# Eight chained sublayers on one core: the norm of a sublayer's first step moved into the sublayer ahead

## The reference

```python
x = x + jnp.tanh(g_xattn[0]) * _L0_xattn_ref(_layernorm(x), ctx_2048, ...)   # A: 32 heads of 8, q and k normed
x = x + jnp.tanh(g_ffn[0])   * _L0_ffn_ref(_layernorm(x), ...)               # B: Hadamard, 8-bit inputs, ternary weights
x = x + jnp.tanh(g_xattn[1]) * _L1_xattn_ref(_layernorm(x), ctx_2048, ...)   # C: norms again, inputs rounded to fp8, two attentions
x = x + jnp.tanh(g_ffn[1])   * _L1_ffn_ref(_layernorm(x), ...)               # D: attention whose tanh(attn @ Wo.T @ A) scales a low-rank gate
x = x + jnp.tanh(g_xattn[2]) * _L2_xattn_ref(_layernorm(x), ctx_2048, ...)   # E: quantised attention over all 1024 keys
x = x + jnp.tanh(g_ffn[2])   * _L2_ffn_ref(_layernorm(x), ...)               # F: 8 experts, 2 chosen, and a shared one
x = x + jnp.tanh(g_xattn[3]) * _L3_xattn_ref(_layernorm(x), ctx_2048, mask)  # G: attention without projections
x = x + jnp.tanh(g_ffn[3])   * _L3_ffn_ref(_layernorm(x), ...)               # H: Hadamard, SiLU gate, Hadamard
```

## Time and profile before

| what | value |
|---|---|
| median of three runs | 1738.55 us (1736.21 to 1738.9) |
| the profiled execution | 1734.91 us, of which the span of the core is 1733.1 us |
| mean granted TensorE clock | 0.823 of full speed |
| TensorE matmul busy | 1374.4 us, 79% of the span |
| VectorE busy | 1217.3 us, 70% |
| ScalarE busy | 958.6 us, 55% |
| GpSimd busy | 277.4 us, 16% |
| DMA | 38.09 MB, mean 22 GB/s |

### The profile page before, as it was taken

The page is one execution under the profiler, slowest core; times in us unless marked ns, Lnnn a source line. Parts: engine busy times, 40 slices in busy tenths (PEclk is TensorE's granted clock), DMA queues, the critical chain, the costliest instruction groups (busy, mean ns, idle before and its releaser), DMA issues.

```text
span 1733.1 us, 26920 instructions
## 1 busy us (share of the span) xinstructions
PE 1374.4 (79%) x9109; PEld 962.1 (56%) x9122; DVE 1217.3 (70%) x2705; ACT 958.6 (55%) x2865; POOL 277.4 (16%) x347
## 2 busy tenths in 40 slices
PE   4775665388898897996799995788888899977886
PEld 3653444156675665675567762444444457765664
DVE  4786887679889999874454418888888885644432
ACT  2552677387687786881456513667766772323121
POOL 0000322143353443442000000000000000000000
PEclk8995787699899999997999998556555558978888
DMA  5302000100000000004200000000000001000000
GB/s 196 144 4 97 1 0 1 52 1 7 1 1 6 1 3 3 1 1 159 98 1 1 1 1 19 1 2 1 0 0 0 1 1 49 0 1 0 1 0 24
DMA packets 13581, 38.09 MB, mean 22 GB/s; under 512 B 2201, under 2 KB 8866, under 8 KB 10802
## 3 DMA queue, kind: packets, MB, share of 16 engines
q1 hardware_dynamic: 13490, 36.99, 5.7%
HBM read 35.94 MB, written 1.05 MB: 21 GB/s over the span
## 4 chain that ended last, share of the span: by engine, by line
PE 47%; DVE 35%; ACT 8%; issue 7%; POOL 2%; DVEq 0%; DMA 0%; ACTq 0%; POOLq 0%; another core or an unknown queue 0%
PE PS L2287 4%; PE PS L2267 4%; PE PS L2899 4%; DVE small L2407 3%; DVE work L1134 2%; DVE work L2417 2%; PE PS L1874 2%; PE PS L1803 2%; PE PS L690 2%; PE PS L1367 2%; PE PS L1905 2%; DVE work L1161 2%; PE PS L2934 2%; PE PS L1375 2%; DVE small L1183 1%
## 5 line engine op out<-in xcount | busy, mean ns | idle before, releaser
L2407 DVE TENSOR_REDUCE small<-PS 128x1 f32<-128x1024 f32 x128 | 156.3, 1221 | 18.1 <-PE PS L2267 12.9
L2352 ACT ACTIVATE work<-PS,small 128x1024 f32<-128x1024 f32 x128 | 154.8, 1209 | 23.9 <-DVE small L2409 23.0
L212 POOL TENSOR_TENSOR rstd<-moments,eps 128x1 f32<-128x1 f32 x56 | 13.5, 240 | 923.2 <-DVE moments L192 923.2
L2287 PE MATMUL PS<-ident_b,work 128*128 128x128 bf16 x1024 | 122.6, 295 | 41.9 <-DVE work L2417 35.5
L1250 POOL TENSOR_TENSOR small<-small,minus_half 128x4 f32<-128x4 f32 x96 | 108.9, 1135 | 263.1 <-ACT small L1290 262.8
L1375 PE MATMUL PS<-late 128*128 128x512 f16 x384 | 103.6, 402 | 58.5 <-DVE work L1177 34.7
L2267 PE MATMUL PS<-early,work 64*128 64x512 bf16 x256 | 121.9, 575 | 4.6 <-ACT work L2352 2.8
L2287 PEld LDWEIGHTS PS<-ident_b,work 128*128 128x128 bf16 x1024 | 92.3, 133 | 47.2 <-DVE work L2417 36.9
L1340 ACT ACTIVATE work<-PS,small 128x128 f32<-128x128 f32 x256 | 90.3, 364 | 48.0 <-DVE small L1184 48.0
L2345 ACT COPY work<-PS 128x512 f32<-128x512 f32 x128 | 75.0, 586 | 68.6 <-PE PS L2287 68.6
L1375 PEld LDWEIGHTS PS<-late 128*128 128x128 f16 x384 | 36.1, 101 | 112.0 <-DVE work L1177 46.7
(11 more groups left out here) (407 smaller groups left out, 3436.4 us busy)
## 6 DMA issues: line engine op xcount, KB each, us to landing
late<-in_C_proj SPq DMA_DIRECT2D x1, 4096.0 KB, 12.4
ctxT<-in_ctxT SPq DMA_DIRECT2D x24, 128.0 KB, 2.6
late<-in_C_q SPq DMA_DIRECT2D x1, 2048.0 KB, 9.1
late<-in_C_qx SPq DMA_DIRECT2D x1, 2048.0 KB, 12.6
late<-in_F_w SPq DMA_DIRECT2D x2, 1024.0 KB
...
```

The costliest lines, as they stand in the source:

```text
L2287: last = nc.tensor.transpose(bank(g, 1).bitcast(BF16)[:, b * P:(b + 1) * P], E_[g]["pb"][:, b * P:(b + 1) * P], ident_b[:])
L2352: nc.scalar.activation(E_[g]["e"], banks(g, 2), ACT.Exp, scale=small[:, g, h:h + 1], bias=small[:, g, 48 + h:49 + h], accum_out=small[:, g ...
L2407: ch.link(nc.vector.tensor_reduce(small[:, g, 80:81], banks(g, 2), AX.X, ALU.max))
```

## The change

The norm of the first step is moved from the beginning of B, C, D, F, G and H into the last step of the sublayer ahead. There it is called with `STEPS` in place of the step, which stands for batches 0 and 1 of X and for the flags of the next sublayer. E's norm stays where it is. In detail:

- A: the buffers are cleared before x is waited for, and TensorE projects the context before it transposes x. In A's last slot the order is now `out_T` of the first half, statistics, `out_T` of the second half, xn, and then the rounding of B's weights.
- B: `C_prepare` goes into slot 5, the statistics of C's first norm into slot 6, the first pass and the second norm into slot 7; `C_proj_low` of parts 14 and 15 goes ahead of the last add. GpSimd's powers go with them. TensorE transposes C's x before it waits for the parts of C's weights.
- C: ahead of the loops only the three roundings of batch 0 are done (k, q, v); those of batch 1 are in slot 0 between `normed_k` and `normed_q`. TensorE waits for each input by itself. In the later steps the roundings go batch by batch too, k, q, v.
- D: the first norm is in slots 6 to 8 of C's last step. The transposes of the fold come before the transposes of x, its copy behind the copies of xT, and its products behind `project_qk`. The waits for the cleared buffers (`prepared`) move to where they are used. `D_xb` lies elsewhere.
- F: its first norm is in slots 8 and 10 of E's last step. G: the statistics of batches 0 to 5 are taken at the head of F's last body, those of 6 and 7 between xn 1 and xn 2. H: its norm is between G's adds.

```diff
-        BEFORE[0, 4] = A_prepare
+        BEFORE[0, 4] = lambda dve, ch: (A_prepare(dve, ch), dve.wait_ge(x_in, 16))
...
             def first(ch):
+                project_kv(0, 0)
                 turn_x(0, 0)
-                projections(0, 0)
+                project_q(0, 0)
                 turn(0, 0, 0)
...
                 if ahead:
                     normed(ch, i, u + 1)
-                elif layers > 1:
-                    B_quantise_weights(dve, ch, PS[:, PREP[0], 0:3])
                 out_T(i, u, 0)
...
+                if not ahead and layers > 1:
+                    norm_stats(ch, STEPS)
                 out_T(i, u, 1)
+                if not ahead and layers > 1:
+                    for b in range(G):
+                        normed_batch(dve, STEPS, b)
+                    B_quantise_weights(dve, ch, PS[:, PREP[0], 0:3])
...
             def first(ch):
-                norm_stats(ch, 0)
-                for u in range(G):
-                    normed_batch(dve, 0, u)
                 norm_stats(ch, 0, [G])
...
+                    if n == 5:
+                        C_prepare(ch)
+                    if n == 6:
+                        norm_stats(ch, STEPS)
+                    if n == 7:
+                        C_again(dve, ch, STEPS)
                 if ahead:
                     quantise_x(ch, i, u + 1)
...
                     if n == 3:
                         C_proj_scale(dve, ch)
+                    if n == NB - 1:
+                        C_twice_normed(dve, STEPS, 0)
                     if n >= 4:
                         for m in (0, 1):
                             C_proj_low(dve, 4 * (n - 4) + m)
+                    if n == NB - 1:
+                        for m in (14, 15):
+                            C_proj_low(dve, m)
                 dve.wait_ge(B_down.sem, B_down.nth(i, u))
                 add_to_x(dve, ch, i * G + u, PS[:, B_DOWN, 0:D], small[:, g, 11:12])
-                if not ahead and layers > 2:
-                    for m in (14, 15):
-                        C_proj_low(dve, m)
...
+                    if n == NB - 2:
+                        norm_gpsimd(pool, ch, STEPS)
+                    if n == NB - 1:
+                        C_again_power(pool, ch, 0)
                     for m in range(3):
                         C_low(pool, 3 * n + m)
...
-        BEFORE[2, 4] = lambda dve, ch: C_prepare(ch)
-        BEFORE[2, 1] = lambda pe, ch: (pe.wait_ge(C_low_done.sem, C_low_done.nth(0, GROUPS - 1)),
+        BEFORE[2, 1] = lambda pe, ch: (C_turn_x(pe, 0), pe.wait_ge(C_low_done.sem, C_low_done.nth(0, GROUPS - 1)),
                                        pe.wait_ge(C_proj_low_done.sem, C_proj_low_done.nth(0, PAIRS - 1)))
...
                 if last_step(i):
+                    if layers > 3:
+                        if n == DEPTH:
+                            norm_stats(ch, STEPS)
+                        if n == DEPTH + 1:
+                            D_normed(dve, ch, STEPS)
+                        if n == DEPTH + 2:
+                            D_normed_again(dve, STEPS, 0)
                     return
...
+                if n == 0:
+                    for k, m in enumerate((2, 0, 3)):
+                        activations(ch, 1, m)
+                        dve.wait_ge(C_xs.sem, C_xs.nth(0, 3 + k))
                 if 1 <= n % UNITS <= G:
                     activations(ch, n % UNITS - 1, 1)
                 if 11 <= n < 17:
-                    m, g = divmod(n - 11, G)
+                    g, m = divmod(n - 11, 3)
                     if m == 0:
                         dve.wait_ge(xT_ready.sem, xT_ready.at(i + 1, g))
-                    activations(ch, g, (2, 3, 0)[m])
+                    activations(ch, g, (2, 0, 3)[m])

             def first(ch):
-                norm_stats(ch, 0)
-                again(ch, 0)
-                twice_normed(ch, 0)
-                for n in (2, 3, 0):
-                    for g in range(G):
-                        dve.wait_ge(xT_ready.sem, xT_ready.at(0, g))
-                        activations(ch, g, n)
+                dve.wait_ge(C_low_done.sem, C_low_done.nth(0, GROUPS - 1))
+                dve.wait_ge(xT_ready.sem, xT_ready.at(0, G - 1))
+                for n, m in enumerate((2, 0, 3)):
+                    activations(ch, 0, m)
+                    dve.wait_ge(C_xs.sem, C_xs.nth(0, n))
...
                 if r == 0:
-                    pe.wait_ge(C_xs.sem, C_xs.nth(i, 8 * (u // UNITS) + 4 + g))
+                    pe.wait_ge(C_xs.sem, C_xs.nth(i, 8 * (u // UNITS) + 3 * g))
...
+                if s == 0:
+                    act.wait_ge(D_folded, 1)
+                    nc.scalar.copy(D_turned_o.rearrange("p a b -> p (a b)"), PS[:, GATE:GATE + 2, :].rearrange("p a b -> p (a b)")).then_inc(D_folded, 1)
...
+                if s == 0:
+                    act.wait_ge(D_folded, 3)
+                    nc.scalar.copy(D_oa.rearrange("p a b -> p (a b)"), PS[:, TBANK_D, 0:64]).then_inc(D_folded, 1)
...
             def turn_x(s):
-                if s >= 2:
-                    pe.wait_ge(x_done.sem, x_done.nth(s - 1, -1))
+                if s != 1:
+                    pe.wait_ge(x_done.sem, x_done.nth(max(s - 1, 0), -1))
...
+            def turn_fold():
+                for k in range(KC):
+                    for tt in range(4):
+                        last = nc.tensor.transpose(PS[:, GATE + k, tt * P:(tt + 1) * P], wD["o"][:, tt, k * P:(k + 1) * P], ident[:])
+                last.then_inc(D_folded, 1)
...
                 if s is not None:
                     project_qk(s)
+                if s == 0:
+                    fold()
...
-            pe.wait_ge(D_folded, 4)
+            turn_fold()
             D_slots(None, slot)
...
                 if last_step(i):
+                    if n == E_DEPTH and layers > 5:
+                        norm_stats(ch, STEPS)
+                    if n == E_DEPTH + 2 and layers > 5:
+                        for b in range(G):
+                            normed_batch(dve, STEPS, b)
                     return
...
             def body(ch, i, s):
-                if s is not None:
+                if i is not None and s is not None:
                     norm_vector(dve, ch, s)
+                if s is None and layers > 6:
+                    G_stats_of(ch, range(6))
...
         def G_vector(dve, ch):
             for h in range(2):
                 dve.wait_ge(rstd_ready.sem, rstd_ready.nth(0, HALF * h + HALF - 1))
                 for b in range(HALF * h, HALF * h + HALF):
+                    if b == 2:
+                        dve.wait_ge(x_done.sem, x_done.nth(0, -1))
+                        G_stats_of(ch, range(6, NB))
...
                     add_to_x(dve, ch, b, PS[:, b, 0:D], G_sum[:, b:b + 1])
+                    if b == G - 1 and layers > 7:
+                        dve.wait_ge(x_done.sem, x_done.nth(0, b))
+                        norm_stats(ch, STEPS)
+                    if b == HALF and layers > 7:
+                        for u in range(G):
+                            normed_batch(dve, STEPS, u)
```

195 lines of the change are left out of this document (107 added, 88 removed).

## The result

The changed kernel took 1692.74 us in the median of four runs (1688.6 to 1700.96), the kernel before 1737.38 in four (1734.19 to 1738.9); the ratio is 0.9752, with an interval of 0.9726 to 0.9777. So 44 us are gone, where 26 were forecast, and the time lies 8 us under the low end of the range, 1701. The profiled execution took 1691.2 us.

A forecast was written before the change was run, and what follows sets the result against it. It took a chain through all engines (47% TensorE, 35% VectorE) to bound the kernel, with waits where sublayers begin. Ten terms summed to -26.2 us, giving 1712 us; own range 1705 to 1719, stretched for rivals to 1701 to 1725.

The forecast's parts named there:

- C's order in the later steps: Middle of C: instructions called the same apart from the order of rounding, with no term for it in the sum.
- A's start: Start of A: buffers cleared before x lands, A_kv's landing late next; -2.9 us.
- A to B: Border of A and B: out_T waits for TensorE and B's weight rounding waits behind it; +0.8 us, bounds -1 to +3.
- B's slots: B's slots 5 to 7: moved constants and norms mostly covered by VectorE's idle time; +1.0 us, bounds 0 to +5.9.
- rival 1: Steps taking in moved work: covers fail, the work costs its length; +12 to +13 us, 1725 us; chance 0.10.
- B to C: Border of B and C: norm done before, three roundings ahead of C's first q; -11.2 us, bounds -8 to -12.5.
- C to D: Border of C and D: q and k projection starts earlier, fold's products ahead of the scores; -7.4 us.
- E's last step: E's last step: VectorE sets the pace, so the added norm is hardly covered; +1.6 us, bounds +0.7 to +2.5.
- E to F: Border of E and F: TensorE's idle time ahead of its first transpose goes; -2.9 us, bounds -3.3 to -2.
- F to G: Border of F and G: statistics of six batches go ahead, first transpose at 1540.6; -4.2 us, bounds -5 and -1.5.
- G to H: Border of G and H: xn ready, but VectorE's adds and H's constants remain; -1.5 us, bounds -2.7 to 0.
- one clock term, at G: G's start: clock stays up because idle time shrinks, products take half as long; up to -8 us, 1704; chance 0.08.

The follow-up runs named there:

- experiments 3 and 4: 3: changed kernel with F's first norm back in F, 32.2 us E's last add to F's first; 4: kernel before plus 18 identity transposes ahead of F, 32.1 us.
- experiment 2: Changed kernel with C's later steps in the old order of rounding; 321.7 us from the add of C's first step to its last's.
- experiment 1: Changed kernel with the load of C_proj sent only after GpSimd's C scale power; B's first add 31.0 us behind B's first maximum, 35.1 without; execution 1701.1 us.
- the first comparison: First profiled execution of the changed kernel, unedited, against that of the kernel before; spans 1689.4 and 1733.1 us.
- the later one: Later execution of the changed kernel, unedited, set against the kernel before; profiled execution 1699.15 us, median of six runs 1692.68 us.
- experiment 9: Changed kernel with C_prepare's constants back at C's start, save one small one; B's fifth and sixth adds 17.4 us apart against 20.0.
- Experiment 10: Changed kernel with six roundings in the old order ahead of C's first step; C's first q 18.4 us behind B's last add against 15.8.

## Why the prediction was wrong

Two steps of the prediction failed. It carried each row's duration over as it stood in the kernel before, at the clock of that row, and so gave F's and D's start no term for the clock's return: 2.4 us at F, shown by experiments 3 and 4, and 2.8 at D, read from the traces. And it put C's order in the later steps at nothing, which is worth 4.7 to 6.0 us (experiment 2). By the borders, in its order:

- **A's start**: right in kind, -3.9 at the squares for -2.9. What was late next was the context (complete at 7.6), not A_kv (7.2), and transposes, copy and q took 1.8 us where I had put 2.9. Another 1.6 came on the way to A's first add, with a granted clock of 0.76 in place of 0.66. But the distance from the squares to that add was 28.8 to 30.5 us in the executions of the changed start, and 30.4 to 30.5 in two of the kernel before, so in two of the twelve this gain isn't there at all.
- **A to B**: right, +0.6 for +0.8, with the idle 4 us where I had put them. My terms behind 143.1 add up to 146.3 and not to 146.9; from the start of out_T to the rounding it took 3.5 us, which is in between. The sentence beside it was wrong: "nobody needs them before about 200". VectorE reads the power in B's first slot, at 176, and I hadn't looked the reader up. It had been just in time before. That costs 4.2 us at B's first add (experiment 1), of which 2.4 are left at the fifth add in the first comparison and nothing in the later one.
- **B's slots**: +1.0 forecast, +4.2 measured. I took the mean idle time of a slot as cover. In slot 5 there was none (2.7, experiment 9), in slot 7 not enough (1.6), and slot 6 cost nothing. This is rival 1, and in B it came true; in C (+0.6) and F (0.0) it didn't.
- **B to C**: -12.6 for -11.2, by the steps named: first rounding to first q 14.8 us for 14.5, first rounding 1.0 us behind B's last add for a forecast of 2.8 behind it. Experiment 10 sizes the order at 2.5.
- **C's order in the later steps**: no term in the sum. I said that in the middle of a sublayer the instructions are the same "apart from C's order of rounding", and then gave this no price. It is worth 4.7 to 6.0 us over three changes of step (experiment 2), the largest single miss. I had read only the first step's start.
- **C to D**: the start was right to 0.2 us. The scores came 11.0 us earlier and not 7.4: 2.8 of the difference is the projection's duration, 9.9 us at half clock in the row that I used and 7.2 in eight of eleven executions with the new code, and 0.8 the fold's products, which cost nothing (the scores start 1.8 us behind the projection's end, 1.6 before). Half clock there had begun ahead of the removed wait, and what lifted it isn't shown. The +2.2 within D is chance: a second execution of the kernel before took 212.2 us there, more than the changed kernel's 211.3.
- **E's last step**: +1.6 forecast. The step itself shows +1.0 up to E's last add but one (64.3 us in all eleven executions with the norm, 63.3 in both without) and +0.4 to +1.0 up to the last. So it cost less than forecast. (1.8 less 0.75 is 1.05 and not the 0.7 of the lower bound.) The -2.5 for E as a whole says nothing, since executions of the same code spread over 7.7 us.
- **E to F**: the wait 2.9, as forecast; 2.4 us of clock beside it (experiments 3 and 4); the rest of the 7.7 a second dip that isn't the norm's, so that wait and clock together are 4.8.
- **F to G**: -4.8 for -4.2. The reading of the clock beside it was wrong. I took the fall to come "about 2 us into the idle time", since the stretch that I read began at 1540, but TensorE stood idle from 1537.1 on:

```profile
1537.10:1542.00 4.90, 0.00 (x0) 0.00 (x0) 4.62 (x14) 0.00 (x0) 0.00 (x0) 1.00 0.01 2
1542.00:1544.80 2.80, 0.00 (x0) 0.01 (x1) 2.63 (x12) 0.00 (x0) 1.50 (x3) 0.50 0.00 0
```

So the fall came 4.9 us behind the start of the idle time. In the changed kernel it came 4.8 us behind it too, at 1506.0, when the wait of 3.6 us was over and G's work had begun; that G kept its half clock was right, and the argument for it was not.
- **G to H**: the first transposes of H come 6.9 us behind G's first add where it was 9.1, so -2.2 for -1.5. The first adds show -2.5 for both times that occur, 65.0 and 69.0 us before, 62.5 and 66.5 changed.

The sum with what was found: -26.2, less 5.2 for the clock at F and D, 4.7 to 6.0 for C's order and 1.4 for C's start, and plus 4.2 and 3.2 for the two costs missed in B, is -30 to -31. The profiled executions differ by 43, the medians by 45. The rest is of the size in which executions of one code differ: E's 4.1 below the forecast, the second dip at F (2.9), A's 1.6, B's middle (1.8). How much of it the change makes isn't shown. The range failed with the steps above: its low end was built from one clock term, at G, which didn't come true.
